# Twelve row places, other groups normalized on GpSimd, a minimum for the clamp, no products without a reader, and new queue orders

## The reference

```python
x = L0_attn_x                                    # (2, 2048, 128)
sa, ca, ga, sb, cb, gb = modulation(silu(c) @ wmod)
h = layernorm(x) * (1 + ca) + sa
# gated linear recurrence over the 2048 positions of each batch
gate_x = sigmoid(block_diag(h, w_in)); gate_a = sigmoid(block_diag(h, w_a))
log_a = -8 * softplus(a_param) * gate_a
y = linear_scan(exp(log_a), sqrt(1 - exp(2 * log_a)) * gate_x * h)
x = x + ga * y
h = layernorm(x) * (1 + cb) + sb
# router: silu(h @ rw1 + rb1) @ rw2 + rb2, the two best of 8 experts, softmax over them
# each token: sum over its two experts of share * (silu(h @ w1[e] + b1[e]) @ w2[e] + b2[e])
return x + gb * experts(h)
```

## Time and profile before

| what | value |
|---|---|
| median of 3 runs | 290.06 us (289.06 to 291.38) |
| profiled execution | 288.09 us, its span 286.2 us |
| mean granted clock of TensorE | 0.956 |
| busy: TensorE, VectorE, ScalarE, GpSimd | 248.1, 188.4, 166.5, 171.6 us |
| TensorE busy between 160 and 240 us | 10.00 of each 10 us |
| ScalarE busy, 80 to 90, 90 to 100, 100 to 110 us | 6.90, 4.49, 5.36 us |
| chain that ended last | PE 40%, POOL 27%, issue 14%, DVE 12%, DMA 4% |

### The profile page before, as it was taken

The page is one execution under the profiler, slowest core; times in us unless marked ns, Lnnn a source line. Parts: engine busy times, 40 slices in busy tenths (PEclk is TensorE's granted clock), DMA queues, the critical chain, the costliest instruction groups (busy, mean ns, idle before and its releaser), DMA issues.

```text
span 286.2 us, 4950 instructions
## 1 busy us (share of the span) xinstructions
PE 248.1 (87%) x1179; PEld 178.0 (62%) x1179; DVE 188.4 (66%) x750; ACT 166.5 (58%) x322; POOL 171.6 (60%) x192
## 2 busy tenths in 40 slices
PE   7767759997599798999999999999999999989910
PEld 6424334444144245687878888888888888868700
DVE  3959999999999987576444444444444446866533
ACT  4189979999785355545555555555555556445300
POOL 4996211267777757777777777644554445645650
PEclk9997979999779799999999999999999999999995
DMA  7993011121131226413533333222217822280505
GB/s 222 308 333 117 19 40 38 37 75 50 55 121 48 89 82 157 114 47 115 149 84 85 111 101 109 57 75 75 74 46 214 221 72 74 84 256 4 161 0 147
DMA packets 45365, 30.51 MB, mean 107 GB/s; under 512 B 5085, under 2 KB 41999, under 8 KB 45342
## 3 DMA queue, kind: packets, MB, share of 16 engines
q1 hardware_dynamic: 40432, 21.75, 27.9%
q0 software_dynamic: 4544, 8.47, 9.0%
q10 hardware_dynamic: 366, 0.04, 0.1%
HBM read 16.39 MB, written 12.67 MB: 102 GB/s over the span
## 4 chain that ended last, share of the span: by engine, by line
PE 40%; POOL 27%; issue 14%; DVE 12%; DMA 4%; POOLq 1%; DVEq 0%; SPq 0%; ACT 0%
POOL sorted_rows L550 21%; PE bank L1218 18%; PE bank L1205 18%; POOL shared L514 3%; PE bank L1226 3%; PE bank L1194 2%; DVE st L698 2%; DMA expert_out<-shared,tx 2%; POOL rs L506 1%; DVE shared L718 1%; POOL expert_out L559 1%; DVE tx L792 1%; DMA xs<-in_L_attn_x_dram 1%; DVE xs L803 1%; DMA tx<-sorted_rows 1%
## 5 line engine op out<-in xcount | busy, mean ns | idle before, releaser
L559 POOL DMA_INDIRECT expert_out<-shared,tx x78 | 80.4, 1031 | 52.9 <-DVE shared L1012 37.4
L657 ACT ACTIVATE hT<-bank,w_t 128x256 f32<-128x256 f32 x156 | 65.4, 470 | 29.3 <-PE bank L1205 28.3
L550 POOL DMA_INDIRECT sorted_rows<-rows,sloti x64 | 63.9, 999 | 27.2 <-issue 18.3
L1205 PE MATMUL bank<-xT,w_t 128*128 128x256 f32 x312 | 74.1, 380 | 0.1
L1218 PE MATMUL bank<-hT,w_t 128*128 128x256 f32 x312 | 74.1, 380 | 0.0
L1205 PEld LDWEIGHTS bank<-xT,w_t 128*128 128x128 f32 x312 | 56.3, 190 | 6.8 <-DVE w_t L995 0.7
L1218 PEld LDWEIGHTS bank<-hT,w_t 128*128 128x128 f32 x312 | 56.2, 190 | 6.2
L666 ACT ACTIVATE yT<-bank,w_t 128x256 f32<-128x256 f32 x39 | 18.4, 473 | 47.6 <-PE bank L1218 47.6
L1134 PE MATMUL bank<-h2T,rw_s 128*128 128x512 f32 x64 | 36.8, 677 | 1.7 <-ACT qv L644 1.4
L986 DVE COPY xT<-bank 128x256 f32<-128x256 f32 x39 | 16.5, 422 | 23.6 <-PE bank L1194 23.6
L1012 DVE TENSOR_TENSOR shared<-bank,tx 128x256 f32<-128x256 f32 x39 | 16.5, 423 | 21.3 <-PE bank L1226 21.2
(11 more groups left out here) (194 smaller groups left out, 328.9 us busy)
## 6 DMA issues: line engine op xcount, KB each, us to landing
tx<-sorted_rows SPq DMA_DIRECT2D x39, 130.0 KB, 2.2
w_s<-in_L_ffn_w_dram SPq DMA_DIRECT2D x16, 256.0 KB, 6.1
xs<-in_L_attn_x_dram SPq DMA_DIRECT2D x8, 256.0 KB, 5.2
rows<-rows SPq DMA_DIRECT2D x8, 256.0 KB, 2.6
av<-expert_out SPq DMA_DIRECT2D x8, 256.0 KB, 3.7
qv<-expert_out SPq DMA_DIRECT2D x6, 256.0 KB, 5.0
expert_out<-shared,tx POOLq DMA_INDIRECT x78, 2.3
sorted_rows<-padr SPq DMA_DIRECT2D x9, 130.0 KB, 3.0
```

The lines of the kernel that those rows point to most:

```text
L550: p.indirect_dma_start(sorted_rows[:, :], bass.IndirectOffsetOnAxis(ap=sloti[:, k, t:t + 1], axis=0), rows[:, t, k, :], None).then_inc(s_d ...
L559: p.indirect_dma_start(expert_out[:, :], bass.IndirectOffsetOnAxis(ap=xr_i[:, s % U, n, D + 1:D + 2], axis=0), yo[:, s % U, n, :], None, b ...
L657: ins = nc.scalar.activation(hsT[:, u % 2, h, :], bank[4 + q][:, (h % 2) * SL:(h % 2 + 1) * SL], ACT.Silu, bias=w1_t[:, u % 2, HID + h:HID ...
L1205: ins = t.matmul(bank[4 + h // 2][:, (h % 2) * SL:(h % 2 + 1) * SL], w1_t[:, u % 2, h * P:(h + 1) * P], xT[:, u % 2, :], start=True, stop= ...
```

## The change

Tiles 0 and 1 get places of their own (10 and 11), so that twelve tiles load before a place is used again; from tile 2 on the place is `s % 10` as before. GpSimd normalizes groups 4, 5 and 6, VectorE the others. For groups 0 to 3 GpSimd takes the minimum of q and 1, and the square root on ScalarE does the scale and the bias. The eleven TensorE products of the identity with itself (`warm`), which nothing reads, are gone. All four plans are new.

```diff
-    FIRST = 11
+    FIRST = 12
+    SLOTS = 12
-    POOLED = 3
+    CLAMPED = 4
+    POOLED = (4, 5, 6)
...
-                warm:0 turnc:0 warm:1 mod:0 warm:2 turn_x:0 gates:0 turnb:0 turn_x:1 gates:1 turn_x:2 turn_x:3 gates:2 turn_x:4 turn_y:0
+                turnc:0 mod:0 turn_x:0 turnb:0 turn_x:1 gates:0 gates:1 turn_x:2 modrow:0 turn_x:3 gates:2 gates:3
...
+                router:27 sum:5 turn_h:7 logits:6 router:28 router:29 router:30 rank:5 router:31 tx:0 sum:6 tx:1 l1:0
+                logits:7 tx:2 rank:6 l1:1 sum:7 l2:0 tx:3 l1:2 rank:7 ty:0 l2:1 tx:4 l1:3 lev:0 ty:1 l2:2 tx:5 l1:4
+                ty:2 l2:3 tx:6 l1:5 count:1 ty:3 l2:4 tx:7 l1:6 ty:4 l2:5 tturn:0 tx:8 l1:7 ty:5 l2:6 l1:8 ty:6 l2:7
...
-                w1:2 xT:2 xT:3 w1:3 w2:1 rowsB:0 sc:0 w2:2 top2:7 xT:4 w1:4 place:7 w2:3 sc:1 w1:5 xT:5 w2:4 table2:0
-                sc:2 w1:6 xT:6 sc:3 xT:7 w2:5 w1:7 w2:6 sc:4 w2:7 xT:8 table3:0 sc:5 w1:8 w1:9 sc:6 w2:8 xT:9 w2:9
+                stats1:0 setup:0 norm1:0+stats1:1 mods:0+stats1:2 norm1:1 stats1:3+soft:0 colsb:0 norm1:2 csilb:0
+                norm1:3+stats1:4 input:0 consts:0+stats1:5 input:1 scan:0 scan:1 resid:0+rowsA:0 input:2
+                resid:1+stats1:6 norm2:0 input:3 scan:2 input:4 scan:3 resid:2+norm2:1 resid:3+scan:4 norm2:2 norm2:3
+                stats1:7+top2:0 input:5 place:0 resid:4 scan:5 top2:1+root:4 norm1:7 resid:5+place:1 input:6 norm2:4
+                root:5+top2:2 scan:6 place:2 resid:6+norm2:5 root:6+top2:3 input:7 norm2:6 place:3 scan:7
+                top2:4+table1:0 resid:7 root:7+place:4 norm2:7 w1:0 top2:5 w2:0 place:5 xT:0 w1:1 top2:6 xT:1 w2:1
+                w1:2 xT:2 place:6 top2:7 xT:3 table1b:0 w1:3 place:7 sc:0 rowsB:0 w2:2 xT:4 w1:4 sc:1 w2:3 xT:5
+                table1c:0 sc:2 w1:5 xT:6 w2:4 w1:6 sc:3 w2:5 xT:7 table2:0 sc:4 w1:7 table3:0 xT:8 w2:6 sc:5 w1:8 w2:7
...
+                ident:0 rstd1:0 wsel:0 rstd1:1 const:0 rstd1:2 rstd1:3 clamp:0 rstd1:4 clamp:1 norm1:4 rstd1:5 norm1:5
+                clamp:2 rstd2:0 clamp:3 rstd1:6 norm1:6 rstd2:1 rstd2:2 rstd2:3 rstd1:7 send:0 send:1 send:2 send:3
...
+        def slot(s):
+            return U + s if s < SLOTS - U else s % U
...
-                if s * HALVES * ROW + HALVES * ROW > GPB * G and s * HALVES * ROW <= GPB * G:
+                if s == 0:
                     sp.wait_ge(s_y, NG)
-                load(s, s % U)
+                load(s, slot(s))
...
+            def no_more_than_one(g):
+                pool.wait_ge(s_exp, g + 1)
+                p.tensor_scalar(qv[:, cols(g)], qv[:, cols(g)], 1.0, None, ALU.min).then_inc(s_up, 1)
...
+                if g < CLAMPED:
+                    act.wait_ge(s_up, g + 1)
+                    nc.scalar.activation(qv[:, cols(g)], qv[:, cols(g)], ACT.Sqrt, bias=gac[:, 2, 0:1],
+                                         scale=-0.25).then_inc(s_m, 1)
```

More of the change, by code:

```diff
@@ L230, in adaln_block @@
         s_out = sem("s_out")
-        s_sc = sems(*(f"s_sc{i}" for i in range(U)))
+        s_sc = sems(*(f"s_sc{i}" for i in range(SLOTS)))
         s_y01 = sems(*(f"s_y01_{g}" for g in range(NG)))
@@ L265, in adaln_block @@
[L265 to L269, removed]
@@ new lines, in adaln_block @@
+                turn_x:4 turn_y:0 turn_y:1 gates:4 turn_x:5 gates:5 turn_h:0 turn_x:6 turn_y:2 router:0 router:1
+                turn_y:3 gates:6 router:2 turn_h:1 router:3 logits:0 router:4 router:5 sum:0 turn_h:2 router:6
+                router:7 rank:0 turn_y:4 router:8 logits:1 router:9 sum:1 turn_h:3 turn_y:5 router:10 router:11 rank:1
+                router:12 logits:2 router:13 turn_x:7 sum:2 router:14 gates:7 turn_h:4 router:15 rank:2 turn_y:6
+                router:16 logits:3 router:17 sum:3 turn_h:5 router:18 router:19 rank:3 router:20 logits:4 turn_h:6
@@ new lines, in adaln_block @@
+                sum:4 count:0 router:21 turn_y:7 router:22 router:23 rank:4 router:24 logits:5 router:25 router:26
+                router:27 sum:5 turn_h:7 logits:6 router:28 router:29 router:30 rank:5 router:31 tx:0 sum:6 tx:1 l1:0
+                logits:7 tx:2 rank:6 l1:1 sum:7 l2:0 tx:3 l1:2 rank:7 ty:0 l2:1 tx:4 l1:3 lev:0 ty:1 l2:2 tx:5 l1:4
+                ty:2 l2:3 tx:6 l1:5 count:1 ty:3 l2:4 tx:7 l1:6 ty:4 l2:5 tturn:0 tx:8 l1:7 ty:5 l2:6 l1:8 ty:6 l2:7
+                tx:9 tx:10 l1:9 ty:7 l2:8 tx:11 l1:10 ty:8 l2:9 tx:12 l1:11 ty:9 l2:10""",
@@ L373, in rounds, with step_slot @@
         def rounds(s, u):
-            return (s - u) // U + 1
+            if static(s) and s < SLOTS:
+                return 1
+            return (s - u) // U + 1 if u >= SLOTS - U else (s - u - U) // U + 1
+        def step_slot(s, u, by):
+            return slot(s + by) if static(s) else (u + by) % U
+        def slot(s):
+            return U + s if s < SLOTS - U else s % U
         def landed(eng, last):
-            for u in range(U):
-                eng.wait_ge(s_sc[u], 16 * HALVES * ((last - u) // U + 1))
+            for u in range(SLOTS):
+                eng.wait_ge(s_sc[u], 16 * HALVES * len([s for s in range(last + 1) if slot(s) == u]))
         @block.sync
@@ L1069, in biases_turn @@
                 t.transpose(bank[7][:, 0:NSB], smallb[:, :], ident[0:NSB, 0:NSB]).then_inc(s_turnb, 1)
-            def keep_warm(n):
-                if n == 0:
-                    pe.wait_ge(s_ident, 1)
-                for _ in range((4, 4, 3)[n]):
-                    t.matmul(bank[4][:, 0:P], ident[:, :], ident[:, :], start=True, stop=True)
             def modulation(_):
```

98 lines of the change are left out of this document (44 added, 54 removed).

## The result

The changed kernel takes 296.95 us (295.86 to 299.17, six executions), the kernel before 290.21 beside it (288.67 to 291.44): ratio 1.024, 95% interval 1.019 to 1.029. The sign and the mechanism at the seam were forecast, the size was not: 6.7 us lost where I had 3.4. In experiments 1, 2 and 5 every kernel, the one before too, took some 330 us, with all engines standing still for stretches between 60 and 175 us; of those runs I use the rows up to place 0, and the ratio with care.

What follows compares the result with a forecast made beforehand. The bound was taken as GpSimd's sends up to the first scatter, then TensorE from tile 10. Late padding +1.6 (twelve places' gain included) and clock +1.8 gave +3.4 on 290.06: 293.5 us, range 288.3 to 297.5.

Steps and rivals of the forecast that it cites:

- part 4: Seam: `pad_i` written 5.1 us later, at 136.35; paddings hold load 9 to 149.0; layer 1 of tile 9 +1.6 us.
- The stop and the half rate (3.8 us, +1.8): Ahead of tile 9 TensorE stands still 3.8 us, then runs at a throttled clock: 1.8 us added.
- part 3: Start of the expert tiles: layer 1 of tile 0 at 110.9, before 111.48; copy `xT:7` ends at 136.2, before 138.3.
- part 2: Front: scan 0 begins 1.5 us sooner, but place 0 ends at 59.1 (before 57.9), first send 1.2 us later.
- My sign against the padding: A second TensorE stop in the first nine tiles would mean VectorE's new order, not the padding, is the bound.
- The norms "3.3 each": Front, GpSimd: the norms of groups 4 and 5 take 3.3 us each, from steps of 821 ns.
- Scan 0 at 24.0, the minimum at 1.4 us: Front: scan 0 begins at 24.0, not 25.57; one GpSimd minimum of 512 columns takes 1.4 us, at most 3.3.
- The sends end within 0.5 us of before: GpSimd's sends start 1.2 us later, but shrinking slot waits let them end within 0.5 us of 143.6.
- Twelve places, up to 1.8 us: Seam: tiles 9 to 11 load without a scatter wait; layer 1 of tile 9 could begin at 149.1, not 150.91.
- Products: Front: without the unread products group 1's gates may run at 1.2 GHz, 0 to +1.8 us on scan 0; taken 0.
- The tail at 0: `combine` of groups 0 to 3 moves one step later: 0 us, range -0.8 to +0.5.
- Rival C: Front loses: minimum at upper price, gates 0 and 1 at 1.2 GHz, norms 4 to 6 late; 297 us, chance 0.10.

Runs made afterwards that it cites:

- experiments 1, 2 and 5: Three rounds: early table and transpose order; parts one by one; minimum returned to ScalarE; the kernel before took 329.74, 331.34 and 331.69 us beside them.
- e11: Changed kernel with `table2`, which writes `pad_i`, moved ahead from behind `xT:7` to behind `w1:5`, and `count:1` earlier on TensorE: 293.96 us, ratio 1.012.
- e9: Changed kernel with groups 4 to 6 normalized on VectorE and `table2` moved ahead to behind `w1:5`: 292.35 us, ratio 1.010 to the kernel before.
- e10: The changed kernel itself, measured and profiled again: 297.31 us, ratio 1.023 to the kernel before.
- e2: Changed kernel with transposes `turn_y:0` and `turn_y:1` ahead of `turn_x:4` in TensorE's order: 339.53 us, ratio 1.030 to the kernel before.
- e1: Changed kernel with `table2` moved ahead to behind `w1:5` and `count:1` earlier on TensorE, first run: 337.66 us, ratio 1.017 to the kernel before.
- e16: Kernel before with twelve places, and GpSimd's minimum replacing ScalarE's clamp for groups 0 to 3: 292.89 us, ratio 1.011 to the kernel before.
- e15: Kernel before with only the twelve places and their longer lead: 289.65 us, ratio 1.001 to the kernel before.
- e13: Changed kernel with the eleven unread products put back: 296.71 us, ratio 1.026 to the kernel before.
- e14: Kernel before without the eleven unread products, second run: 289.62 us, ratio 0.997 to the kernel before.
- experiment 3: Round measuring the changed kernel, early table, norms on VectorE, and both repairs; the kernel before took 289.66 us beside them.
- e4: Kernel before with only `table2` moved later, behind `xT:7` and `w2:5`: 337.0 us, ratio 1.025 to the kernel before.
- e5: Kernel before without the eleven unread products, first run: 330.67 us, ratio 1.001 to the kernel before.

## Why the prediction was right in sign and wrong in size

- **The padding takes over (part 4).** Right, shown by e11 and e9: `pad_i` behind `xT:7`, SP waiting for a padding, tile 9 late. From `pad_i` to the load of tile 9 I had 12.65 us; e10 took 13.15 (140.55 to 153.70).
- **The stop and the half rate (3.8 us, +1.8).** Right: 4.46 and 0.61 us of waits, and 1.6 us more for layer 1 of tile 9 (3.45 against 1.89). In e11, which has no such stop, there is no half rate; by that the rule of the Trainium skill cited there (TensorE: Matmul & The Clock Gate, "What's actually happening") agrees with the runs.
- **When `pad_i` is written (136.35): the term that failed.** e10 wrote it at 140.55, 4.2 us later, after at 144.09. The lateness is there when the tiles start: layer 1 of tile 0 began at 115.2 where part 3 had 110.9, and from there to `pad_i` it took 25.4 us, as forecast. Of the front, place 0 ended at 62.6 where part 2 had 59.1: 1.4 us of that ahead of scan 0, 2.1 between it and place 0. With 0.5 us more for the paddings and 0.7 more from the load to layer 1, tile 9 began at 157.92 instead of 152.5: 7.0 us behind before, where the sum had 1.6. In the profiled execution after tile 0 began at 118.5, with a second stretch at half rate behind a stop ahead of the last transposes of h2 (TensorE, after):

```profile
109.02 1.11 PE L1077 MATMUL bank<-ident,rows 128*128 128x128 f32 x4 [2.52 <-DVE rows L843]
110.06 1.94 PE L1156 MATMUL bank<-av,rw_s 128*32 128x512 f32 x8
111.93 4.42 PE L1149 MATMUL bank<-h2T,rw_s 128*128 128x512 f32 x6
```

  In e10 the same stop was as long and the full rate followed; six router products took 3.09 us:

```profile
108.29 0.66 PE L1077 MATMUL bank<-ident,rows 128*128 128x128 f32 x4 [2.50 <-DVE rows L843]
```

  My sign against the padding, a second stop within the first nine tiles, does not speak of this one: it lies ahead of tile 0, and behind it TensorE waited no more than 0.5 us until tile 9.
- **The norms "3.3 each" (part 2), mis-sized.** Measured 5.28, 3.14 and 5.01 us. I took the mean of before, 821 ns a step, from steps that ran mostly beside statistics of one input, and moved them beside scans. The group of the page after gives 1130 ns:

```profile
L525 POOL TENSOR_SCALAR shared<-xs,mv,rs 128x128 f32<-128x128 f32 x12 | 13.4, 1130 | 0.2
```

- **What is queued behind the norm: left out.** I named what stands behind the clamps on GpSimd, but not that on TensorE `turn_y:0` stands behind `turn_x:4`. e2 shows it: residual 0 at 28.78 against 31.27, of which 0.6 us arrived at place 0 (e1 against e2).
- **Scan 0 at 24.0, the minimum at 1.4 us.** The minimum is right, 1.50. Scan 0 began at 24.50 in after and at 25.41 in e10, where the gates of group 0 began at 13.9 and not at 12.8; the 1.1 us won ahead of it in after were lost again ahead of residual 0. That GpSimd's minimum slows VectorE, as in e16, I had not priced at all; in the new order it falls on other work.
- **"The sends end within 0.5 us of before": wrong.** Scatter 0, right behind the last send, started at 146.91 in e10 and at 143.89 before: a first send 4.9 us later (63.09 against 58.18) left 3.0 at the end, and the gaps took up 1.9.
- **Twelve places, up to 1.8 us: mis-sized** at 0.3, for the reason read from e15.
- **Products: right at 0** for the time (e13, e14). Without them group 0's gate pairs took 1.92 us each in e10, group 1's 1.25 and 1.02.
- **The tail at 0: right** within a microsecond. From layer 1 of tile 9 to the end the traces of before and after differ by 1.8 us, of which 1.3 is its half rate.

In medians of experiment 3 the changed kernel stood 7.65 us above before: the late table gives back 3.35, the norms on VectorE 2.4, both 5.0, and of the 2.7 left most is the place of the early table. Rival C had the size (297). Of its three causes one was right, the norms of groups 4 to 6 late on GpSimd; the minimum was cheap, and the gates of group 1 ran at full rate but for 0.2 us. It had nothing of a larger loss at the seam, so its number is partly luck.

## What to carry to other kernels

Price a moved instruction by rows in which the same neighbour was busy with the same kind of work, not by its mean. When a helper engine's result feeds an in-order queue, look at what stands behind it there: finished work queued after it waits too, though here most of that wait was taken up before place 0. A chain of DMAs that one small write releases (here 13 us from `pad_i` to the next load) belongs as early as its inputs allow, but not ahead of a step that the busiest engine waits for: here that cost 1.9 us of the gain. Read a loss stage by stage before giving a remainder to what no run has moved.

## What was not expected of the hardware

- GpSimd's 128x128 step of one tensor input went from 0.79 to 1.32 us (3.14 and 5.28 us for four) while VectorE ran products and scans with two inputs; VectorE's scan went from 1.23 to 1.36 us. Beside GpSimd's minimum VectorE's own norm, with one tensor input, went from 1.11 to 1.60 us for four steps. The Trainium skill (GPSIMD Engine Reference, Specifications) lists GpSimd's interfaces to SBUF as shared with VectorE, with contention when VectorE is in a two-port mode or has two SBUF inputs; the rows beside products and scans agree, and the sizes, 1.7 and 1.4 times, are those of the rows. Whether VectorE's norm, with its one tensor input, is in such a mode no run here shows. That rule, weighed ahead of the run, would have cast doubt on the 821 ns, but it gives no size.
- How long TensorE had stood still did not settle its rate afterwards. Stops of 1.51 and 3.19 us (e15, e4) were followed by full rate, 1.02 us a gate pair; stops of 3.05, 3.19 and 3.89 us (e14, e5, e16) by half, 1.91 or 1.92; and the same kernel went both ways behind 2.50 and 2.52 us (e10, after).
